# One block of 64x64 products per chunk in a gated linear attention layer: heads 8 to 15 lag a step, k and the gates join the block, and the second phase turns 64 rows at a time

## What is computed

```python
q, k, v = elu(xn @ Wq) + 1, elu(xn @ Wk) + 1, xn @ Wv      # 16 heads of 64
a = sigmoid(xn @ Wa + ba + 2.0)                            # a decay per row and head
def step(carry, inp):                                      # row after row
    S = at[..., None, None] * S + kt[..., :, None] * vt[..., None, :]
    z = at[..., None] * z + kt
    num = einsum('bhk,bhkv->bhv', qt, S)
    den = einsum('bhk,bhk->bh', qt, z) + eps
    return (S, z), num / den[..., None]
x = x + out @ Wo
x = x + (layernorm(x) @ CB.T) * (SCB / 127) + bias
```

## Time and profile before

| | us |
|---|---|
| median of 3 runs | 2151.82 (2150.62 to 2156.57) |
| profiled execution | 2153.45 |
| its span | 2151.6 |
| phase 1, to the last steps | up to about 1500 |
| phase 2 | about 1530 to the end |
| PE busy | 2101.4 (98%) |
| DVE busy | 1525.4 (71%) |
| ACT busy | 624.3 (29%) |
| POOL busy | 330.0 (15%) |

### The profile page before, as it was taken

How to read it: one execution, slowest core, us unless ns; L and a number is a source line. 1 busy time by engine, 2 the same in 40 slices (tenths; PEclk the granted TensorE clock), 3 DMA queues, 4 the chain that set the end, 5 groups by cost and what they waited for, 6 DMA issues and landing times. The chain is left out here.

```text
span 2151.6 us, 65649 instructions
## 1 busy us (share of the span) xinstructions
PE 2101.4 (98%) x26856; PEld 1810.1 (84%) x26856; DVE 1525.4 (71%) x3393; ACT 624.3 (29%) x1190; POOL 330.0 (15%) x364
## 2 busy tenths in 40 slices
PE   7999999999999999999999999999899999999998
PEld 6888888888888888888888888888688888888887
DVE  7787887777777777778777878876655555555554
ACT  5333333333333333333333333333211111111111
POOL 2111113111112211111221111220100000000000
PEclk9999999999999999999999999999999999999999
DMA  5333334333433343333333343333423323333332
GB/s 190 98 96 104 93 89 103 103 84 99 107 84 89 103 103 90 104 97 84 102 102 90 96 107 87 89 104 106 132 103 117 110 105 114 108 109 112 104 115 74
DMA packets 182029, 220.75 MB, mean 103 GB/s; under 512 B 25184, under 2 KB 107616, under 8 KB 181984
## 3 DMA queue, kind: packets, MB, share of 16 engines
q1 hardware_dynamic: 181984, 220.11, 35.7%
HBM read 168.59 MB, written 51.44 MB: 102 GB/s over the span
## 5 line engine op out<-in xcount | busy, mean ns | idle before, releaser
L1051 PE MATMUL G<-w_hi,xT_hi 128*128 128x512 f32 x1024 | 414.6, 405 | 13.3 <-ACT kT L619 11.7
L1051 PE MATMUL G<-w_hi,xT_lo 128*128 128x512 f32 x1024 | 400.6, 391 | 3.6 <-DVE qT L810 3.3
L1051 PE MATMUL G<-w_lo,xT_hi 128*128 128x512 f32 x1024 | 401.0, 392 | 0.0
L602 ACT ACTIVATE relu_t<-G 128x512 f32<-128x512 f32 x256 | 153.1, 598 | 622.8 <-PE G L1051 622.8
L1051 PE MATMUL G<-xT_lo,w_hi 128*128 128x256 f32 x1024 | 289.8, 283 | 0.0
L1051 PE MATMUL G<-xT_hi,w_lo 128*128 128x256 f32 x1024 | 289.8, 283 | 0.0
L1051 PE MATMUL G<-xT_hi,w_hi 128*128 128x256 f32 x1024 | 289.4, 283 | 0.0
L1051 PEld LDWEIGHTS G<-w_hi,xT_hi 128*128 128x128 f32 x1024 | 192.6, 188 | 67.5 <-ACT kT L619 28.2
L1051 PEld LDWEIGHTS G<-w_hi,xT_lo 128*128 128x128 f32 x1024 | 192.5, 188 | 51.8 <-issue 9.7
L1051 PEld LDWEIGHTS G<-w_lo,xT_hi 128*128 128x128 f32 x1024 | 193.0, 188 | 33.6
L1019 PE MATMUL DS<-w_hi 128*128 128x512 f32 x512 | 206.5, 403 | 0.4 <-issue 0.4
(11 more groups left out here) (136 smaller groups left out, 3847.7 us busy)
## 6 DMA issues: line engine op xcount, KB each, us to landing
abc<-decay_rows SPq DMA_DIRECT2D x256, 128.0 KB, 2.9
pbc<-decay_rows SPq DMA_DIRECT2D x128, 256.0 KB, 4.3
attn_rows<-attn SPq DMA_DIRECT2D x256, 128.0 KB
at_rows<-attn_rows SPq DMA_DIRECT2D x64, 512.0 KB, 3.3
xt<-in_x SPq DMA_DIRECT2D x64, 256.0 KB, 4.2
x_in<-in_x SPq DMA_DIRECT2D x64, 256.0 KB, 3.5
out_rows<-xt SPq DMA_DIRECT2D x64, 256.0 KB, 2.1
xT_in<-in_xT SPq DMA_DIRECT2D x31, 512.0 KB, 3.5
```

What stands on the lines that cost most here:

```text
L602: act.activation(relu_t[j][:, :], bank[:, :], ACT.Relu)
L1051: made = nc.tensor.matmul(to, lhs, rhs, start=(n == 0), stop=(n == len(passes) - 1))
```

## The change

- Phase 1 has **one block per chunk**. Heads 8 to 15 lag a step: step i does delta of heads 8 to 15 for chunk i-1 and their numerators for chunk i-2, scores of heads 0 to 7 for chunk i and of heads 8 to 15 for chunk i-1, delta of heads 0 to 7 for chunk i, and their numerators for chunk i-1. Phase 1 has two more steps at its end for this.
- k is turned at the head of that block, 64 rows at a time (`halves_turned`), into `SC`; ACT copies it in two halves by stretches. k is held once instead of twice.
- The logits of two chunks are made in the block of every second step, by 16 plain fp32 64x64 matmuls from `xT_in` (not the split parts), in spare columns of `DS`. DVE adds the two halves (`logit_sums`), and `decays` works once for both chunks, on 128 partitions.
- ACT copies the numerators out of `NUM` (`num_sb`), and `normalised` reads the copy.
- Each group in the block has its own waits, against registers that count up (`due`, `begin`).
- The order of units becomes k1, v1, then q and k0, v0 of the next chunk; the weights are split in another order at the start, behind each other's units (`order`, `split_lo`).
- Stores of attention rows and the loads of `pbc` go by halves of heads. x's load, norm and spread move by a step.
- In phase 2 the twelve turns stand together, as 24 turns of 64 rows.

```diff
-        order = [NP, 0, NP + 1, 2 * NP, 2 * NP + 1, 1]
+        order = [NP, 0, 2 * NP, NP + 1, 2 * NP + 1, 1]
...
+            def halves_turned(to, j, rows):
+
+                turned = []
+                for a in range(2):
+                    ps = slice(64 * a, 64 * a + 64)
+                    turned.append(nc.tensor.transpose(to[a][:, L * j:L * j + L], rows[ps, 128 * j:128 * j + 128],
+                                                      ident[ps, ps]))
+                return turned
...
-                if b == 1 and exists(i) and exists(i + 1):
-                    x_lo(1, pairs[1], xT_in[:, :, tokens(1)])
-                if here:
-                    decay_matrix(1, d32[0], one[-1])
...
+                if exists(i):
+                    weighted_v(0, one[0], one[-1], b)
+                if exists(i - 1):
+                    state(1)
+                if exists(i - 2):
+                    normalised(1)
+                for r in (1, 0):
+                    if exists(i - r):
+                        masked(r)
+                if gates:
+                    logit_sums()
+                if exists(i):
+                    state(0)
+                for r in (1, 0):
+                    if exists(i - r):
+                        scaled_q(r)
+                if gates:
+                    decays()
+                    if not first:
+                        x_lo(0, pairs[1], xT_in[:, :, tokens(0)])
+                if normal:
+                    x_stats(x16[1])
...
+                if second:
+                    split_lo(3)
+                if exists(i):
+                    elu_k(1, 0)
+                    if second:
+                        split_lo(4)
...
+                def k0_unit():
+
+                    if b == 1:
+                        wait(pe, exp_k_ready[1], one[0])
+                        pe.wait_ge(xT_lo_ready[0], pairs[1])
...
+                if b == 1 and exists(i + 1):
+                    store_decays()
+                    if not exists(i):
+                        sp.wait_ge(w_lo_ready, KT)
+                    spread_decays(0, coming)
+                wait(sp, qs_ready[1], one[-1] if exists(i - 1) else None)
+                wait(sp, qs_ready[0], one[0] if exists(i) else None)
+                wait(sp, pc_ready, one[0] if exists(i) else None)
+                if exists(i):
+                    spread_products(1, this)
+                if exists(i + 1):
+                    spread_products(0, coming)
```

More of the change, by code:

```diff
@@ L663, in step, with copy_kT @@
-                copy_v(1)
+                c32 = counts(act, i, 32, (0, 1))
+                first, second = isinstance(i, int) and i == -1, isinstance(i, int) and i == 0
+                G0, G1 = G
+                def copy_kT():
+                    act.wait_ge(kT_ready, one[0])
+                    held = slice(0 if exists(i) else GH, PT if exists(i - 1) else GH)
+                    for a in range(2):
+                        act.activation(kT[:, held, stretch(a)], turned_k[a][:, held, :], ACT.Copy)\
+                            .then_inc(kT_copied[a], 1)
@@ L1037, in step @@
             def step(i, pair, b):
-                one = counts(pe, i, 1, (-1, 0, 1))
-                pairs = counts(pe, pair, 1, (0, 1))
-                start = not exists(i)
-                here = exists(i)
-                ahead = exists(i + 1)
-                wide = b == 1 and ahead
-                o = 1 - b
-                def product(to, passes, before_last=None):
+                one = counts(pe, i, 1, (-2, -1, 0, 1))
+                pairs = counts(pe, pair, 1, (-1, 0, 1))
+                o = 1 - b
@@ L1093, in q_unit, with unit @@
+                def unit(bank, slab_of, s, ready):
+                    weights(slab_of)
+                    product(bank[:, :], [(xp[:, kt, tokens(s)], w[:, slab_of, kt, :]) for kt, xp, w in parts])\
+                        .then_inc(ready, 1)
+                def q_unit(bank, u):
+                    weights(u * QT // KT)
                     for j in range(QT):
@@ new lines, in v0_unit @@
+                def v0_unit():
+                    if b == 1:
+                        pe.wait_ge(exp_q_ready[0], pairs[1])
+                    else:
+                        pe.wait_ge(exp_q_ready[3], pairs[0])
+                    unit(G1, 2 * NP, o, v_unit_ready[0])
+                if exists(i) or exists(i - 1):
+                    transposes()
+                if exists(i - 2):
+                    carried(1)
+                if exists(i - 1):
+                    delta(1)
+                if exists(i - 2):
+                    within(1)
@@ L1268, in step2 @@
+                if isinstance(i, int) and i == NC + 1:
+                    inputs_of_rows(1, 32)
+                    transpose_rows(1)
+            steps(pe, step, -1, NC + 2)
             def step2(i, _, b):
```

1055 lines of the change are left out of this document (555 added, 500 removed).

## The result

The changed kernel takes 2203.03 us (median of 4 runs, 2201.94 to 2206.24) against 2151.26 for the kernel before, measured beside it: a ratio of 1.0238 (95% interval 1.0217 to 1.0258), 2.4% slower. The profiled execution took 2204.02, with a span of 2202.2.

The account below looks back on a forecast made before the run. PE, busy 98%, was taken to bound the kernel, as far as the others can follow. 2153.5 + 31 (pairs: 3.0 gained, 4.0 of waits) - 16 (phase 2) + 20 (start) = 2188 us, range 2132 to 2255.

Parts of the forecast that it names:

- PE's gain: Phase 1 on PE: fewer blocks, k's turn, logits and waits for q give 3.0 us a pair of chunks.
- the start and the end: Weight splits on DVE stand in series with units, 7 + 7 + 5, plus two extra steps: +20 (+5 to +30).
- sequencer: PE's block in phase 1: some twenty more waits and counts cost nothing (0 to 0.3 a chunk).
- Half turns: k's turn in PE's block: 16 turns of 64 columns a chunk, 0.059 a couple, 0.47 a chunk.
- third rival: Half turns cost as much as whole ones, 0.11, in phase 1 and phase 2: 2250; chance 0.14.
- The low part of x: Step with gates: PE's third unit waits for DVE's serial chain up to the low part, 1.5 a pair.
- x normal: Step with gates: PE's logits wait for POOL's normalised x, 0 to 1.2, taken as 0.7 a pair.
- T: Point from which the prediction times its chains: the end of the group delta of heads 8 to 15.
- The state: Both steps: delta of heads 0 to 7 waits for DVE's state, 0.3 and 0.2 to restart: 1.0 a pair.
- The late products: Products spread late hold ACT's copy of the factors, and the next block waits 0 to 2, taken as 0.8.
- fourth rival: The spread sets the pace: 1.5 a pair instead of 0.8, ACT's lateness reaching the state's wait: 2235; chance 0.13.
- first rival: The blocks pay: DVE's chain keeps ahead, a pair has 1.0 of waits against 3.0: 2090; chance 0.18.

Follow-up runs that it names:

- e7: The changed kernel with two more waits, on constants long reached, ahead of each group in the looped steps: 2206.01 us, ratio 1.0234.
- e5: The changed kernel with DVE's gates step reordered: first low part of x, decays, both qs; second low part ahead of the normalisation: 2165.21 us, ratio 1.0046.
- e3: The changed kernel with the low part of x for a pair's first chunk ahead of the decays on DVE: 2208.75 us, ratio 1.0255.
- e6: The changed kernel with the sums of x ahead of both qs, moments ahead of second qs and normalisation, in the step without gates: 2278.78 us.
- e9: The changed kernel with early splits, e5's order, e6's early sums, ACT's factors behind the second q unit, SP's moments ahead of product spreads: 2164.15 us.
- e1: The kernel before with the changed phase 2 alone, phase 1 untouched: 2139.75 us, ratio 0.9934.
- e2: The changed kernel with the splits of the weights at the start moved earlier, all into step -1: 2176.91 us, ratio 1.0107.
- e4: The changed kernel with eight more steps at the start written out instead of looped: 2228.66 us, ratio 1.0345.
- e10: The changed kernel with early splits, e5's order, ACT's factors behind the second q unit, moments of x inside the normalisation, SP's order unchanged: 2132.03 us.

## Why the prediction was right, point by point

The forecast was slower, 2188 in 2132 to 2255; it came to 2203. Direction and mechanism held. Of the terms of its sum, three were off: PE's gain in a pair was put 0.9 too high, the waits of a pair 1.1 too high, and the start and the end 26 too low. That the pair came out 0.8 longer, against 1.0 forecast, is luck in part, since the first two cancel: the forecast waits with the gain as measured would have made it 1.9 longer, the forecast gain with the waits as measured 0.1 shorter.

**PE's gain.** The step without gates, which never waits, is the clean measure: 21.84 against 23.36, twice 1.52 = 3.04. With the logits, 0.90 a pair (forecast 0.94), that leaves 2.1. Forecast was 3.0. The missing 0.9 is the *sequencer* term, put at nothing: groups in the block start 0.49 to 0.59 apart instead of 0.47 (the 0.61 behind the last has the way out in it), 0.44 a step where the range was 0 to 0.3, and e7 shows that of a further instruction ahead of each group 0.08 of 0.106 is paid in the step without gates. The argument for nothing, that before two groups stood without a gap although a register was counted between them, didn't carry over to a wait or two with each count. It costs the pair little only because PE's waits behind it shrink.

**Half turns.** 16 in 0.64 with the way in, so 0.50, 0.062 a couple against 0.059. The third rival (0.11) is out, in the block and in phase 2. The way in of 0.14 is paid once: from the turns to the next group no third one shows, `carried` behind the turns takes 0.52 (711.68 to 712.20) as the other `carried` does in the step without gates. The Trainium skill (TensorEngine Tiling (Array Packing), Key Properties) has the engine drained at each change of the tiling mode; from 64x128 to 64x64 no run here shows it. The Trainium skill (TensorE: Matmul & The Clock Gate, LDWEIGHTS (loading the stationary operand)) has a load go by the columns that its weights fill. For one load the trace agrees, 0.139 for 64 rows by 128 columns and 0.140 for 128 by 128. But two half turns, side by side, cost little over half of a whole one, so the length of a load does not set their pace.

**The low part of x.** Forecast 1.5 a pair; PE's units are 1.57 longer in the step with gates, 1.31 of it idle in the row. DVE's chain from the second mask (718.05) to the low part (724.73) takes 6.7, where the sum had 0.6 + 0.6 + 1.66 + 1.2 + 1.97 + 0.69 = 6.7. e5 shows that it was this chain. What the forecast did not see is what stands right behind it: e3 takes the wait away from this place and gains nothing.

**x normal.** Forecast 0.7, measured 0.8. The reason given, DVE's sums behind 10 us of its own work (9.9 measured from T to the moments) and spread and POOL behind them, is what the trace shows: SP waits 0.7 a pair for the moments. What it left out is SP's order, with `qs` and the spread of the products 0.7 behind the moments as the next in line; e6 and e9 ran into that.

**The state.** Forecast 0.5 in both steps, measured 0.5 in the step with gates and none in the other. In the other step state begins when delta is done, and the four groups, 2.16 instead of 1.88 since they are slower, cover it. In the step with gates the weighted v stands ahead and takes 1.13 beside POOL, so the term was right in size there for another reason.

**The late products.** Forecast 0.8 a pair, measured nothing on PE: ACT does wait for `pbc` (56 us), but it is absorbed. It takes little more, decays 0.6 later, to reach the state, as e3 shows; so the fourth rival is not what the changed kernel does, but it is what e3 and e9 ran into. Together the waits are 2.9 a pair instead of 4.0, and the pair is 0.8 longer instead of 1.0.

**Phase 2.** Forecast -16, measured -16 (9.55 to 9.27 a step), and e1 has it alone (-14).

**The start and the end.** This is the term that was mis-sized: +20 (5 to 30) against 37 + 9. The mechanism was right for the splits (7 + 7 + 5 forecast; five waits of 24.4 measured, 28 gained by e2, of it some 7 by the clock). Two costs were not seen at all: TensorE's clock falls in these waits, and the joined block starves for instructions in steps that are written out, 14 us. Neither was among the rows on which the forecast rested. e2 and e4 measure both.

The first rival (2090, the blocks pay) was not absurd: with DVE's order repaired, a pair does gain, 45.9 against 46.7 in e10, which is at 2132. Its condition, that 1.5 fall out of DVE's chain ahead of the low part, is just what e5 met by order instead of by speed.

## What to carry to other kernels

When a stage of the critical engine is made shorter, write the other engines' chains from one fixed point to each of its waits, with the queue that issues the transfers as one of the engines; here the change was worth 2 us a pair on PE, order on DVE decided whether it was gained or lost, and a single call on SP was worth 36. If one wait is removed, ask for the next two before counting the gain. Cost a start by itself, and look whether an engine's dense stretch of small instructions lies in code that isn't looped.

## What the runs showed of the hardware

- A joined block of 64x64 matmuls, some 600 instructions in 5 us, stalls for 0.3 to 4.6 in nearly every step where the code is written out, and never in the changed kernel's loop; with wide products between the groups the same number of written-out steps costs next to nothing (0.5 waited). The stalls end 1.3 to 1.6 behind the landing of a 16 KB block of instructions, and these blocks come no closer than 3.4 us in any trace.
- Half turns of 64 rows, two side by side, cost 0.062 a couple against 0.11 for a whole one.
- TensorE's clock was granted at 0.54 in the 4 us behind an idle stretch of 6.8, and products of 512 columns then start 0.43 apart instead of 0.23.
- For the landing of one small store SP waits 2.2 where it is issued straight behind four spreads of 128 KB (e10), 1.6 where 0.7 lie between (changed kernel), and 1.3 ahead of them (e9).
- Some of DVE's instructions that stay in SBUF are longer while POOL works: scan 1.22 to 1.88, weighted v 0.70 to 1.13, a small one 0.16 to 0.81. So where POOL's passes fall in the step is a cost of its own. The Trainium skill (SBUF — State Buffer, SBUF: two separate sides) has the two engines lock each other out of a shared pair of ports for a whole instruction, and the trace agrees: an instruction is longer by what is left of the other engine's, not by a factor. This pass of POOL, 0.86 where it is alone, ends at 713.27:

```profile
711.61 1.67 POOL L597 TENSOR_TENSOR xT_in<-xT_in,bias_b 128x256 f32<-128x256 f32 x1
```

  The weighted v begins at 712.70 and ends at 713.83, which is its own 0.70 behind the end of that pass, less 0.14. The same 0.14 comes out for k (709.46 to 710.80), the scan (710.72 to 712.61) and the small one (715.41 to 716.22) with the passes that they met, which end at 710.25, 711.53 and 716.19. POOL's three stretched passes fit DVE's ends alike, less 0.13 to 0.20.
